# Third layer of a graph network: the join moved into the next step and alternated with the links of the sum, and other orders of steps on the engines

## The reference, cut to what matters

```
m = relu(feat[src]) + EPS
ex = exp(m - seg_max[dst])
denom = segment_sum(ex, dst)
msg = segment_sum(ex / denom[dst] * m, dst)
out = (feat + msg) @ W + b
x = layernorm(x + out)
```

## Time and profile before

| | us |
|---|---|
| median of 3 runs | 3799.91 (3792.94 to 3800.45) |
| the profiled execution, its own time | 3788.51 |
| its span, first to last instruction | 3786.7 |
| busy in the whole span: PE, DVE, ACT, POOL | 1847.8, 2821.7, 1853.3, 2675.7 |
| the third layer's stage in the span | about 2176 to 2773 |

### The profile page before, as it was taken

How to read it: one execution, slowest core, us unless ns; L and a number is a source line. 1 busy time by engine, 2 the same in 40 slices (tenths; PEclk the granted TensorE clock), 3 DMA queues, 4 the chain that set the end, 5 groups by cost and what they waited for, 6 DMA issues and landing times. The chain is left out here.

```text
span 3786.7 us, 39744 instructions
## 1 busy us (share of the span) xinstructions
PE 1847.8 (49%) x8382; PEld 1354.4 (36%) x8382; DVE 2821.7 (75%) x10541; ACT 1853.3 (49%) x3815; POOL 2675.7 (71%) x2760
## 2 busy tenths in 40 slices
PE   5478675888766666744554357888820000000000
PEld 2244313777755555522222157777710000000000
DVE  8899987888866666659999878888755565555555
ACT  8699602776652222225545546666643333333333
POOL 7377776777747777757777477766457777777776
PEclk9899855888878787766666656665655555555555
DMA  2111397666556666646666545555422222222221
GB/s 53 51 41 40 79 295 200 168 166 162 156 139 201 205 205 210 203 131 204 208 202 210 167 156 173 185 171 171 147 82 78 82 77 78 82 74 81 82 73 55
DMA packets 380539, 524.64 MB, mean 139 GB/s; under 512 B 221914, under 2 KB 255983, under 8 KB 380042
## 3 DMA queue, kind: packets, MB, share of 16 engines
q1 hardware_dynamic: 286154, 366.89, 29.3%
q0 software_dynamic: 94144, 155.21, 17.4%
HBM read 230.36 MB, written 291.54 MB: 138 GB/s over the span
## 5 line engine op out<-in xcount | busy, mean ns | idle before, releaser
L1626 POOL DMA_INDIRECT l_G<-t,src x391 | 387.7, 991 | 181.8 <-issue 150.8
L1927 POOL DMA_INDIRECT l_G<-t,src x391 | 373.3, 955 | 168.3 <-issue 107.4
L2161 PE MATMUL l_psR<-l_diag,l_ones 128*128 128x128 f32 x2 | 0.8, 501 | 991.2 <-DVE l_diag L2025 991.2
L1307 POOL DMA_INDIRECT l1a_G<-t,src x391 | 378.8, 969 | 148.3 <-issue 117.3
L1307 POOL DMA_INDIRECT l1b_G<-t,src x391 | 378.4, 968 | 142.8 <-issue 117.9
L1942 POOL DMA_INDIRECT out<-O,nidx x392 | 384.3, 980 | 127.8 <-issue 118.2
L642 POOL DMA_INDIRECT O<-x_pad,nidx x344 | 326.9, 950 | 104.7 <-issue 104.7
L973 POOL DMA_INDIRECT l_G<-xs,src x327 | 311.7, 953 | 99.6 <-issue 96.3
L2161 PEld LDWEIGHTS l_psR<-l_diag,l_ones 128*128 128x128 f32 x2 | 0.5, 310 | 991.3 <-DVE l_diag L2025 991.3
L207 ACT ACTIVATE O<-O,l_shift,l_rstd 128x96 f32<-128x96 f32 x784 | 291.2, 453 | 27.2 <-DVE l_shift L201 26.7
L1480 PE MATMUL l1b_psE<-l1b_G,ident 128*128 128x384 f32 (+1 forms) x198 | 147.1, 845 | 260.3 <-DMA l1b_G<-t,src 260.3
(11 more groups left out here) (351 smaller groups left out, 6480.8 us busy)
## 6 DMA issues: line engine op xcount, KB each, us to landing
h<-l_G SPq DMA_DIRECT2D x96, 392.0 KB, 2.9
t<-l1b_t_out SPq DMA_DIRECT2D x48, 768.0 KB
h<-l_G SPq DMA_DIRECT2D x48, 768.0 KB
xs<-en_y SPq DMA_DIRECT2D x48, 392.0 KB, 4.3
t<-l_t_out SPq DMA_DIRECT2D x48, 392.0 KB, 3.6
l_H<-t SPq DMA_DIRECT2D x48, 392.0 KB, 3.2
en_y<-x_pad SPq DMA_DIRECT2D x48, 384.0 KB, 5.0
t<-l_tr_out SPq DMA_DIRECT2D x48, 384.0 KB
```

The source lines that it names most:

```text
L1307: pool.indirect_dma_start(tile(c)[:, q, :], None, table, bass.IndirectOffsetOnAxis(k.src[:, at:at + 1], 0))\
L1626: pool.indirect_dma_start(tile(c)[:, q, :], None, table, bass.IndirectOffsetOnAxis(k.src[:, at:at + 1], 0))\
L1927: pool.indirect_dma_start(tile(c)[:, q, :], None, t4, bass.IndirectOffsetOnAxis(k.src[:, at:at + 1], 0))\
```

## The change

DVE's `join` is split. Its multiplication becomes `divide`, at the head of the next step. Its eight additions are made in that step too, one after each link of the following chunk's sum (`chain_and_join`), in steps 1 to 47; in step 0 and from step 48 on chain and join stay apart, join now working on chunk t-1. `factors` moves to the next step's head, `measure` stands behind the paired block. ACT and PE get a new order of work within a step, in which `turn_v`, `copy_v` and `mix` handle t-1 in the step of the join, and `take` and the write to `t4` come at t-4 in place of t-5. The operations themselves, their sizes and their number are the same, but for one drain fewer or more at the edges.

```diff
@@ sync
-                for c in due(t - 5, LATE):
+                for c in due(t - 4, LATE):
                     u, n = c % 2, width(c)
                     sp.wait_ge(taken, c + 1)
                     sp.dma_start(part_of(t4, c), t_out[:, u, 0:n, :]).then_inc(stored[u], 16)
@@ vector
+            def link(c, q):
+                S, at = tile(c), STARTS[c] + q
+                if at:
+                    if q and at > 1:
+                        dve.wait_ge(linked, links(c, q - 1))
+                    before = S[:, q - 1, :] if q else tile(c - 1)[:, width(c - 1) - 1, :]
+                    done = dve.scalar_tensor_tensor(S[:, q, :], before, k.cont[:, at:at + 1], S[:, q, :],
+                                                    ALU.mult, ALU.add)
+                    done.then_inc(linked if q < width(c) - 1 else chained, 1)
+
+            def join_tile(c, q):
+                u, at = c % 2, STARTS[c] + q
+                done = dve.scalar_tensor_tensor(inv[:, u, q, :], inv[:, u, q, :], k.lastok[:, at:at + 1],
+                                                k.O[:, at, :], ALU.mult, ALU.add)
+                if q == width(c) - 1:
+                    done.then_inc(joined, 1)
...
+            def chain_and_join(c):
+                dve.wait_ge(gathered.of(c), gathered.by(c))
+                dve.drain()
+                for q in range(width(c)):
+                    link(c, q)
+                    join_tile(c - 1, q)
...
-            def join(c):
-                u, n = c % 2, width(c)
-                v = inv[:, u, 0:n, :]
+            def divide(c):
+                v = inv[:, c % 2, 0:width(c), :]
                 dve.wait_ge(inverted, c + 1)
                 dve.tensor_tensor(v, v, tile(c)[:, :, D:W2], ALU.mult)
...
             for t in range(LAST + 1):
+                paired = 1 <= t < NCH - 1
+                for c in due(t - 1, LATE):
+                    divide(c)
+                for c in due(t - 3, LATE):
+                    factors(c)
                 for c in entering(t):
-                    chain(c)
+                    if paired:
+                        chain_and_join(c)
+                    else:
+                        chain(c)
+                if t == NL:
+                    close()
+                if not paired:
+                    for c in due(t - 1, LATE):
+                        join(c)
                 for c in due(t - 2, LATE):
                     measure(c)
-                if t == NL:
-                    close()
-                for c in due(t, LATE):
-                    join(c)
-                for c in due(t - 2, LATE):
-                    factors(c)
                 for c in due(t - 5, LATE):
                     take_own(c)
@@ scalar
             for t in range(LAST + 1):
+                for c in due(t - 3, LATE):
+                    apply(c)
+                for c in due(t, LATE):
+                    invert(c)
+                for c in due(t - 4, LATE):
+                    take(c)
                 for c in due(t - 1, LATE):
                     copy_v(c)
-                for c in due(t - 5, LATE):
-                    take(c)
-                for c in due(t - 4, LATE):
-                    copy_x(c)
-                for c in due(t, LATE):
-                    invert(c)
-                for c in due(t - 3, LATE):
-                    apply(c)
                 for c in due(t - 2, LATE):
                     root(c)
+                for c in due(t - 3, LATE):
+                    copy_x(c)
@@ tensor
             for t in range(LAST + 1):
-                for c in due(t - 1, LATE):
-                    mix(c)
                 for c in due(t - 4, LATE):
                     multiply(c)
-                for c in due(t - 3, LATE):
-                    turn_x(c)
-                for c in due(t, LATE):
+                for c in due(t - 1, LATE):
                     turn_v(c)
                 if t == NCH:
                     pe.wait_ge(chained, NL)
                     pe.matmul(sums, k.carry_from[:, :], tile(NL - 1)[:, width(NL - 1) - 1, :], start=True, stop=True)\
                       .then_inc(carried, 1)
+                for c in due(t - 3, LATE):
+                    turn_x(c)
+                for c in due(t - 1, LATE):
+                    mix(c)
```

More of the change, by code:

```diff
@@ L1642, in _ @@
             dve.tensor_copy(w4[0:D, D:D + 2], psX[0:D, 0:2]).then_inc(widened, 1)
+            def link(c, q):
[13 more added lines that the diff above has]
+                    done.then_inc(joined, 1)
             def chain(c):
-                S = tile(c)
                 dve.wait_ge(gathered.of(c), gathered.by(c))
@@ L1663, in close, with join @@
                 dve.tensor_tensor(F[:, 0, :], F[:, 0, :], carry[:, :], ALU.add).then_inc(chained, 1)
-            def join(c):
-                u, n = c % 2, width(c)
-                v = inv[:, u, 0:n, :]
+            def divide(c):
+                v = inv[:, c % 2, 0:width(c), :]
                 dve.wait_ge(inverted, c + 1)
                 dve.tensor_tensor(v, v, tile(c)[:, :, D:W2], ALU.mult)
+            def join(c):
+                n = width(c)
+                v = inv[:, c % 2, 0:n, :]
                 dve.drain()
@@ L1672, in join @@
                     for q in range(n):
-                        at = STARTS[c] + q
-                        last = dve.scalar_tensor_tensor(inv[:, u, q, :], inv[:, u, q, :], k.lastok[:, at:at + 1],
-                                                        k.O[:, at, :], ALU.mult, ALU.add)
-                else:
-                    last = dve.tensor_tensor(v, v, k.O[:, span(c), :], ALU.add)
-                last.then_inc(joined, 1)
+                        join_tile(c, q)
+                else:
+                    dve.tensor_tensor(v, v, k.O[:, span(c), :], ALU.add).then_inc(joined, 1)
             def measure(c):
```

## The result

| | kernel before | changed |
|---|---|---|
| median, us | 3797.81 (5 runs) | 3823.86 (5 runs, 3816.66 to 3827.46) |
| profiled execution, us | 3788.51 | 3826.75 |
| its span, us | 3786.7 | 3825.0 |

The ratio is 1.0072, 95% interval 1.0059 to 1.0084. The forecast was 3768.7, in a range of 3753 to 3792. The two profiled executions lie 38 us apart, the medians 26; what follows compares the two traces and so explains 38.

A forecast was written before the change was run, and what follows sets the result against it. POOL waited for `chained` at DVE's pace, 11.20 us a step. POOL's 10.38 plus 0.17 for PE's half clock made 10.55; 48 x (11.20 - 10.55) = 31.2, tail 0, so 3799.9 - 31.2 = 3768.7 us, range 3753 to 3792.

The forecast's parts named there:

- POOL bound by `chained` at DVE's pace: Third layer before the change: POOL's gathers wait for slots freed by DVE's chain; 32 us of waiting over 295 gaps.
- DVE's pauses by the inverse behind the copy that waits for TensorE: ACT inverts only after `copy_v`, which waits for PE's transposes; DVE's waits on ACT come to 79 us, 1.6 a step.
- The two waits: DVE's waits for ACT's inverse (50.5 us) and 1/deviation (28.7 us): the first should go, the second shrink to about nothing.
- my estimate of 0.59 a pair: DVE's paired block: link 0.35 plus addition 0.24 us, overlapping, so eight pairs take 4.7 us.
- rival 3: Pairing hides nothing: 0.73 us and more per pair, DVE's step 10.7, above POOL's; total 3776; chance 0.10.
- The slack of 3 us: POOL's slot loop takes 17.3 us for two steps that last at least 20.5, so freeing slots later costs nothing.
- Rivals 1 and 2: PE's half clock bounds the step at 11.2 us (3799.9, chance 0.12); PE's queue at 11.5 slows it (3814, chance 0.05).
- The 0.17 us that I added for PE's half clock: Added to POOL's 10.38 us step for stretches with PE at 11.2, where DVE falls behind by 0.8 a step.
- the 1.20 us ahead of the gather at 2413.11: Read as POOL starting 1.20 us late, 0.7 behind a chain's end, to show that it waits for `chained`.
- The multiplication is still made once a chunk, so I keep the later stretch's 0.992: POOL's gather stays at 0.992 us, not the early 0.978, giving 8 x (0.992 + 0.306) = 10.38 us a chunk.
- the tail: The 47.4 us from closing chain to layer four's first gather; claimed change 0 with +-4.
- The rival that ended slower: ACT's root behind `copy_v`, `turn_v` and `multiply`: PE's round 11.5 us on half clock, +14 us, 3814; chance 0.05.

The follow-up runs named there:

- e8_act_order: The kernel before with ScalarE's order alone changed: inverse, then root, ahead of the copies, take and apply; 3746.03 us, ratio 0.9884.
- e7_mid_drain: The changed kernel with one drain of DVE in the middle of the block, behind the fourth pair; 3752.39 us, ratio 0.9894.

## Why the prediction was wrong

**Right.** POOL bound by `chained` at DVE's pace, and DVE's pauses by the inverse behind the copy that waits for TensorE: e8_act_order alone shows it. The two waits go; POOL's gap falls from 0.414 to 0.305. The pair overlaps: 4.56 us a block against 4.7 from my estimate of 0.59 a pair. So rival 3 falls. The rule that I quoted for it from the Trainium skill (VectorE: DVE Perf Modes, section "The DRAIN you can't avoid") was half of what stands there: the section goes on that a next operation that isn't held starts earlier, and the 0.08 us of overlap agree with that half. The slack of 3 us holds: POOL never waits for a slot. Rivals 1 and 2 fall: TensorE's granted clock is 0.69 over the stretch, and PE's busy share 64%. The 0.17 us that I added for PE's half clock has nothing to answer to, since POOL's gap is 0.305 throughout. One reading was loose: the 1.20 us ahead of the gather at 2413.11 are its whole gap, 0.9 more than usual.

**Wrong, the step that failed: "The multiplication is still made once a chunk, so I keep the later stretch's 0.992".** The gather's duration in the new kernel was 1.197. I asked of POOL only whether its slots come free in time, and whether the one instruction that I had seen holding it up would run more often. I didn't ask what else the rewritten block is to POOL. Yet the row was there: L1669, two SBUF tensors, held the gather at 2415.61 to 0.82 us behind its end; the links and additions have two SBUF tensors as well. Before, VectorE paused 0.03 us behind each link, and a run of additions ended after 1.92 us, so no gather was issued over 1.5 us into a run. The change removed the pauses and made the run 4.56 us. I had worked these 0.03 us out as DVE's gain. With the hold of 1.64 us a step put into the sum, 10.38 + 1.64 = 12.02, against a measured 12.01; that closes the account of the step, but it is no forecast, since the hold is read from the same trace.

Without that hold the forecast would have stood, by some luck: e1_apart, the same orders without alternation, ran in 3757.24 where I had said 3768.7, its step 10.67 where I had said 10.55. Its steps gave 25 us where I had said 31, and 6 came from the tail, which I had put at nothing.

**A smaller miss, the tail.** "0 with +-4": it was -7.8. All versions with the new orders have it (38.8 to 42.6 us), and those with the old ones don't (44.9 to 50.4). So the orders make it. Which of them, wasn't tried.

**The rival that ended slower** named the wrong queue. None of mine had POOL itself slow down.

## What to carry to other kernels

Where an engine issues indirect DMAs one after the other and is near the bound, its time for each is a quantity that the other engine's instructions can change; look what VectorE does in the rows around the longest of them before you count a packed VectorE as a gain. A short pause in a long run of two-input VectorE instructions can be worth far more than it costs: here a pause that makes the block 0.16 us longer takes away holds of 1.6 us a step. And before a restructuring, try the cheap half of it: the order of one in-order engine gave the full gain by itself.

## What the runs showed of the hardware

- An indirect DMA issued by GpSimd while VectorE works through an unbroken run of instructions with two SBUF tensors can be held until the run ends. Of 169 gathers of seven kernels that were issued in such a run and took over 1.3 us, 166 ended 0.81 to 0.83 us behind the end of the run; a gather usually lasts 0.95 us.
- Two things go with such a long hold. One is how long the run has lasted at the issue: in the changed kernel's 4.56 us blocks none of 57 gathers within 2.0 us took over 1.3 us, 45 of 53 later did; in others some did from 1.4 us on (ten at 1.54 us in e1_apart, six at 1.77 in e7_mid_drain). The other is the moment within VectorE's instruction: over 2.0 us into a run, 151 of 153 issued within 0.11 us of an instruction's start were held beyond that instruction, and none of 30 issued later in it (four kernels). The commonest held gather was issued 2.33 us into the block, 0.09 us behind a link's start. Why it takes both stays open.
- A single instruction with two SBUF tensors holds a gather too, from its start and to its own end: L1669, 0.96 us long, the gather issued 0.08 us into it, and 131 of 131 gathers issued 0.05 to 0.6 us into it in the eleven traces. The early gathers of a run were also held to the end of the one instruction in which they were issued, which cost them 0.21 us at most in the changed kernel.
- Batch-norm statistics between the links, which read one tensor, break the long hold, and an addition of 128x768 with its second input in PSUM holds nothing (157 gathers, none over 0.95 us). The Trainium skill (SBUF — State Buffer, section "Who interferes with whom") states that a VectorE instruction with two SBUF inputs contends with a GpSimd instruction that reads SBUF, and infers that descriptor generation isn't touched. I had read that, in the prediction, as leaving these gathers out, and the rows as showing otherwise. But each gather takes its row numbers from `src`, which this kernel keeps in SBUF, so it reads SBUF, and the rule for reads may be the one at work; no run here parts this reading from the other. That the wait lasts until the one instruction has ended agrees with the section's exclusive lock; that it can last through a whole series of instructions isn't stated there.
